# Weighting the experts' hidden layer straight from PSUM on VectorE, output sum on VectorE, third layer four experts behind

## What is computed

```python
x = x + conv(_ln_c(x), w_qkv, w_out, b_out)        # linear attention, 8 heads of 32
t = tokens(x)                                      # [16, 1024, 128]
z = _ln_t(t)
feat = mean(z, axis=0)                             # over the images: [1024, 128]
w = softmax(feat @ Wr + br)                        # [1024, 8]: one weight per pixel and expert
h = relu(bn(z @ W1[e] + b1[e]))                    # for each of 8 experts, hidden 128
h = relu(bn(h @ W2[e] + b2[e]))
y = sum_e w[:, e] * (h @ Wo[e] + bo[e])
x = t + y
```

## Time and profile before

| | |
|---|---|
| device time, median of 3 runs | 882.08 us (880.58 to 882.58) |
| span of the profiled execution | 879.8 us (first to last instruction; the page has no other time of this execution) |
| TensorE busy | 814.8 us, 93% |
| VectorE busy | 738.1 us, 84% |
| ScalarE busy | 575.7 us, 65% |
| GpSimd busy | 340.3 us, 39% |
| mean granted TensorE clock | 0.979 |
| chain of waits: TensorE, VectorE, ScalarE | 52%, 13%, 2% |

### The profile page before, as it was taken

One profiled execution on the slowest core, in us unless ns is written; L12 is line 12 of the kernel. 1 busy time (PEld: TensorE's weight loads), 2 busy tenths in 40 slices (PEclk: granted clock), 3 DMA queues, 4 the chain that ended last, 5 costly groups with the idle time before them and its releaser, 6 DMA issues.

```text
span 879.8 us, 12875 instructions
## 1 busy us (share of the span) xinstructions
PE 814.8 (93%) x4170; PEld 673.9 (77%) x4170; DVE 738.1 (84%) x1165; ACT 575.7 (65%) x650; POOL 340.3 (39%) x377
## 2 busy tenths in 40 slices
PE   5899999999998898899999999999898998999997
PEld 4899999999975677687877878777686776877775
DVE  5678888888866788989898898988989889898887
ACT  2456566666555676767767767676676767767665
POOL 5548787878753221404123041331403214042120
PEclk8999999999999999999999999999999999999999
DMA  7133434343422501201011010110101002010000
GB/s 223 49 121 144 144 137 150 134 152 111 155 96 89 200 24 48 72 1 72 8 63 72 0 72 0 72 58 13 72 0 72 35 37 72 0 72 24 24 25 24
DMA packets 22107, 64.52 MB, mean 73 GB/s; under 512 B 2608, under 2 KB 6840, under 8 KB 22080
## 3 DMA queue, kind: packets, MB, share of 16 engines
q1 hardware_dynamic: 22080, 64.19, 20.4%
HBM read 38.98 MB, written 25.20 MB: 73 GB/s over the span
## 4 chain that ended last, share of the span: by engine, by line
PE 52%; DVE 13%; issue 3%; ACT 2%; POOL 0%; DVEq 0%; ACTq 0%; POOLq 0%
PE psum L515 51%; DVE h_lo L899 9%; DVE w_raw L893 3%; ACT h L691 2%; DVE st L849 0%; PE psum L472 0%; PE psum L566 0%; DVE xn2T L779 0%; POOL ln L989 0%; DVE h_lo L882 0%; POOL xn2T L997 0%; DVE x_res L954 0%; DVE w_raw L933 0%; ACT h_hi L698 0%; PE psum L424 0%
## 5 line engine op out<-in xcount | busy, mean ns | idle before, releaser
L899 DVE TENSOR_TENSOR h_lo<-w_raw,h_hi 128x1024 fp32r<-128x1024 f32 x128 | 219.3, 1714 | 1.1 <-ACT h_hi L698 1.1
L684 ACT ACTIVATE h_hi<-psum 128x1024 fp32r<-128x1024 f32 x128 | 131.5, 1027 | 122.7 <-PE psum L515 122.7
L515 PE MATMUL psum<-h_hi,w_hi 128*128 128x512 f32 x510 | 164.9, 405 | 41.0 <-DVE h_lo L899 41.0
L882 DVE SCALAR_TENSOR_TENSOR h_lo<-psum,h_hi 128x1024 fp32r<-128x1024 f32 x128 | 156.4, 1222 | 42.0 <-ACT h_hi L684 41.7
L1040 POOL TENSOR_TENSOR x_res<-y_out,x_res 128x1024 f32<-128x1024 f32 x15 | 41.1, 2737 | 380.3 <-ACT y_out L734 380.3
L893 DVE TENSOR_TENSOR w_raw<-h,route_all 128x1024 f32<-128x1024 f32 x127 | 160.1, 1261 | 30.5 <-ACT h L691 30.5
L691 ACT ACTIVATE h<-psum,t 128x1024 f32<-128x1024 f32 x128 | 143.1, 1118 | 49.1 <-PE psum L515 49.1
L515 PE MATMUL psum<-h_lo,w_hi 128*128 128x512 f32 x510 | 164.1, 404 | 0.0
L515 PE MATMUL psum<-h_hi,w_lo 128*128 128x512 f32 x510 | 162.9, 401 | 0.0
L515 PEld LDWEIGHTS psum<-h_hi,w_hi 128*128 128x128 f32 x510 | 94.4, 190 | 74.5 <-DVE h_lo L899 51.8
L698 ACT CAST h_hi<-w_raw 128x1024 fp32r<-128x1024 f32 x128 | 132.9, 1039 | 1.6 <-DVE w_raw L933 1.2
(11 more groups left out here) (130 smaller groups left out, 1159.7 us busy)
## 6 DMA issues: line engine op xcount, KB each, us to landing
route_all<-in_x SPq DMA_DIRECT2D x16, 512.0 KB, 4.1
x_res<-in_x SPq DMA_DIRECT2D x16, 512.0 KB, 3.4
x_scratch<-x_res SPq DMA_DIRECT2D x16, 512.0 KB, 2.9
xn_scratch<-xn SPq DMA_DIRECT2D x16, 512.0 KB, 2.6
xs_in<-xn_scratch SPq DMA_DIRECT2D x16, 512.0 KB, 4.5
x_res<-x_scratch SPq DMA_DIRECT2D x16, 512.0 KB, 3.3
out<-x_res SPq DMA_DIRECT2D x15, 512.0 KB, 2.6
route_all<-route_scratch SPq DMA_DIRECT2D x6, 512.0 KB, 6.6
```

What stands on the lines that cost most here:

```text
L515: mm = pe.matmul(dst[:, px], w[:, which, e, :], part[:, px], start=first and w is w_hi and part is hi, stop=last and part is lo, skip_grou ...
L684: nc.scalar.activation(h1_hi[r][:], z1[r], ACT.Relu).then_inc(h1_hi_done, 1)
L882: nc.vector.scalar_tensor_tensor(out=h1_lo[r][:], in0=z1[r], scalar=0.0, in1=h1_hi[r][:].bitcast(F32), op0=ALU.max, op1=ALU.subtract).then ...
L899: nc.vector.tensor_tensor(h2_lo[r][:], h2w[r], h2_hi[r][:].bitcast(F32), ALU.subtract).then_inc(h2_lo_done, 1)
```

## The change

It does this:

- `hidden2` is gone. `weigh` reads z2 in PSUM and makes max(z2, -t2) * route in one scalar_tensor_tensor on VectorE. Since max(z, -t2) = relu(z + t2) - t2, the third layer lacks t2 * route @ Wo; it is put back in the bias: `shifts_through_wo` (8 small matmuls, once) gives t2 @ Wo of each expert, and `bo_full` = bo + that is used in place of bo. Layer2 of a slot now waits for `weigh` of the slot before (h2w_done).
- In the bridge z2 of experts 0 and 1 is copied to SBUF by ScalarE (`z2_out`), since no routing weights exist yet; the product for the bias goes to y's banks and the order is another.
- The output sum is one VectorE tensor_tensor from PSUM at the head of the fifth slot of an image; ScalarE's copy of y and GpSimd's `finish` are gone. Layer3 of the next image waits for it (out_done).
- layer3 runs four slots behind, and h2w, h2_hi and h2_lo are rings of four, which use tiles of the attention stage.
- GpSimd keeps `split_low` and `bias_x1`, now in its own loop over slots; it also makes -t2 and the operand of the 8 small matmuls.

The diff, without the constants and the list of semaphores:

```diff
--- before.py
+++ after.py
...
@@ -72,7 +72,8 @@
     SLOTS = IMAGES * EXPERTS
-    L3_LAG = 3
+    L3_LAG = 4
+    RING = 4
     SPREAD = 2
     BRIDGED = 4
     x1_dram = nc.dram_tensor("x1_scratch", [IMAGES, C, PIXELS], F32, kind="Internal").ap()
@@ -97,7 +98,10 @@
         w_lo = sb("w_lo", [128, 3, EXPERTS, 128], F32R)
         ident = sb("ident", [128, 128])
         t2 = sb("t2", [HIDDEN, EXPERTS])
+        minus_t2 = sb("minus_t2", [HIDDEN, EXPERTS])
+        t2_diag = sb("t2_diag", [HIDDEN, EXPERTS, EXPERTS + 1])
         bo_sb = sb("bo_sb", [EXPERTS, C])
+        bo_full = sb("bo_full", [EXPERTS, C])
         wr_sb = sb("wr_sb", [C, EXPERTS])
         br_sb = sb("br_sb", [128, EXPERTS])
         feat = sb("feat", [128, CHUNKS, C])
@@ -231,13 +235,11 @@
         xs_lo = [sb(f"xs_lo{p}", [C, PIXELS], F32R) for p in range(2)]
         h1_hi = [sb(f"h1_hi{p}", [HIDDEN, PIXELS], F32R) for p in range(2)]
         h1_lo = [sb(f"h1_lo{p}", [HIDDEN, PIXELS], F32R) for p in range(2)]
-        h2 = [sb(f"h2_{p}", [HIDDEN, PIXELS]) for p in range(2)]
-        h2w = [w_raw[:, p].rearrange("p e h -> p (e h)") for p in range(2)]
-        h2_hi = [sb(f"h2_hi{p}", [HIDDEN, PIXELS], F32R) for p in range(2)]
-        h2_lo = [sb(f"h2_lo{p}", [HIDDEN, PIXELS], F32R) for p in range(2)]
-
-        y_out = sb("y_out", [C, PIXELS])
-        feat_most = y_out
+        z2_early = [sb(f"z2_early{p}", [HIDDEN, PIXELS]) for p in range(2)]
+        feat_most = sb("feat_most", [C, PIXELS])
+        h2w = [w_raw[:, p].rearrange("p e h -> p (e h)") for p in range(3)] + [feat_most[:]]
+        h2_hi = [sb(f"h2_hi{p}", [HIDDEN, PIXELS], F32R) for p in range(2)] + xn_hi
+        h2_lo = [sb(f"h2_lo{p}", [HIDDEN, PIXELS], F32R) for p in range(2)] + xn_lo
         z1, z2, y = [banks(4, 2), banks(6, 2)], banks(0, 2), banks(2, 2)
         xs_loaded = [sem(f"xs_loaded{p}") for p in range(2)]
...
@@ -398,6 +401,8 @@
                     mm.then_inc(m_done, 1)
                 if b:
                     turn_e(t, 0, 0)
+                if at(t, 0):
+                    shifts_through_wo()
                 if s:
                     pe.wait_ge(in_loaded[p], 8 * t + (24 if p else 32))
@@ -463,6 +468,14 @@
                                    start=False, stop=True)
                 mm.then_inc(shift_done, 1)
+            def shifts_through_wo():
+
+                pe.wait_ge(t2_ready, 1)
+                for e in range(EXPERTS):
+                    mm = pe.matmul(p_g[0:EXPERTS, 256:384], t2_diag[:].rearrange("p e f -> p (e f)")[:, 8 * e:8 * (e + 1)],
+                                   w_raw[:, 2, e, :], start=e == 0, stop=e == EXPERTS - 1)
+                mm.then_inc(wo_t2_done, 1)
+
             def turn(dst, chunk):
                 return turn_part(dst, 128, chunk)
@@ -500,6 +513,8 @@
             def add_g(t, p, j, h):
                 pe.wait_ge(e_moved, 4 * t + 2 * j + h + 1)
+                if isinstance(t, int) and t == j == h == 0:
+                    pe.wait_ge(bo_full_done, 1)
                 for n in range(4):
                     chunk = 4 * h + n
                     mm = pe.matmul(p_g[:, 128 * j:128 * (j + 1)], xnT[p][:, chunk, :], ekT[j][:, chunk, :],
@@ -525,15 +540,20 @@
             def layer2(s, k):
                 pe.wait_ge(h1_lo_done, s + 1)
-                wait(pe, h2_done, s)
+                if isinstance(s, int) and s <= 2:
+                    wait(pe, z2_moved, s)
+                else:
+                    pe.wait_ge(h2w_done, s)
                 layer(z2, 1, k % EXPERTS, h1_hi[k % 2], h1_lo[k % 2], True, True).then_inc(l2_done, 1)
             def layer3(s, k, image):
-                e, r = (k - L3_LAG) % EXPERTS, (k - L3_LAG) % 2
+                e, r = (k - L3_LAG) % EXPERTS, (k - L3_LAG) % RING
                 pe.wait_ge(h2_lo_done, s - L3_LAG + 1)
-                if e == 0:
-                    wait(pe, y_out_moved, image)
+                if isinstance(s, int) and s == L3_LAG:
+                    pe.wait_ge(bias_moved, 1)
+                elif e == 0:
+                    pe.wait_ge(out_done, image)
                 if isinstance(s, int) and s == SLOTS - 1 + L3_LAG:
                     for n in range(2):
@@ -571,17 +591,13 @@
             turn_part(y, EXPERTS, lambda n: route[:, n, :]).then_inc(routeT_done, 1)
             turn(z1[0], lambda n: route[:, n, 0:1].to_broadcast([128, 128])).then_inc(spread, 1)
+            layer2(2, 2)
             pe.wait_ge(routeT_moved, 1)
             turn(y, lambda n: route[:, n, 1:2].to_broadcast([128, 128])).then_inc(spread, 1)
-
-            pe.wait_ge(h2_done, 2)
+            pe.wait_ge(spread_moved[1], 1)
             for n in range(2):
-                mm = pe.matmul(z2[:, BANK * n:BANK * (n + 1)], bo_sb[:], routeT[:, BANK * n:BANK * (n + 1)], start=True, stop=True)
+                mm = pe.matmul(y[:, BANK * n:BANK * (n + 1)], bo_full[:], routeT[:, BANK * n:BANK * (n + 1)], start=True, stop=True)
             mm.then_inc(bias_done, 1)
-            pe.wait_ge(spread_moved[1], 1)
-            layer3(3, 3, 0)
-            pe.wait_ge(bias_moved, 1)
-            layer2(2, 2)
             pe.wait_ge(spread_moved[0], 1)
             def slot(s, k, image):
@@ -683,18 +699,16 @@
                 wait(act, l2_done, s - 1)
                 nc.scalar.activation(h1_hi[r][:], z1[r], ACT.Relu).then_inc(h1_hi_done, 1)
-            def hidden2(s, k):
-
-                r, e = k % 2, k % EXPERTS
+            def z2_out(s):
+
                 act.wait_ge(l2_done, s + 1)
-                wait(act, h2w_done, s - 1)
-                nc.scalar.activation(h2[r][:], z2, ACT.Relu, bias=t2[:, e:e + 1]).then_inc(h2_done, 1)
+                nc.scalar.copy(z2_early[s][:], z2).then_inc(z2_moved, 1)
             def h2_high(s, k):
-                r = k % 2
+                r = k % RING
                 act.wait_ge(h2w_done, s + 1)
-                wait(act, l3_done, s - 1)
+                wait(act, l3_done, s - RING + 1)
                 nc.scalar.copy(h2_hi[r][:], h2w[r]).then_inc(h2_hi_done, 1)
             rounds(act, step)
@@ -703,39 +717,31 @@
             h1_high(0, 0)
             last_round(step, IMAGES + 1)
             h1_high(1, 1)
-            hidden2(0, 0)
+            z2_out(0)
             act.wait_ge(turned, 1)
             nc.scalar.mul(feat_most[:], p_chan, 1.0 / IMAGES).then_inc(feat_most_moved, 1)
             h1_high(2, 2)
             act.wait_ge(feat_moved, 1)
             last_round(step, IMAGES + 2)
-            hidden2(1, 1)
+            z2_out(1)
             act.wait_ge(step_done, 3)
             nc.scalar.activation(grown[:].rearrange("p n e -> p (n e)"), shifted[:].rearrange("p n e -> p (n e)"), ACT.Exp).then_inc(grown_done, 1)
+            h1_high(3, 3)
             act.wait_ge(routeT_done, 1)
             nc.scalar.copy(routeT[:], y[0:EXPERTS, :]).then_inc(routeT_moved, 1)
-            h2_high(0, 0)
+            act.wait_ge(spread, 1)
+            nc.scalar.copy(route_all[:, 0, :], z1[0]).then_inc(spread_moved[0], 1)
             act.wait_ge(spread, 2)
             nc.scalar.copy(route_all[:, 1, :], y).then_inc(spread_moved[1], 1)
+            h2_high(0, 0)
             act.wait_ge(bias_done, 1)
-            nc.scalar.copy(bias_out, z2).then_inc(bias_moved, 1)
-
-            nc.scalar.copy(route_all[:, 0, :], z1[0]).then_inc(spread_moved[0], 1)
-            h1_high(3, 3)
-            hidden2(2, 2)
+            nc.scalar.copy(bias_out, y).then_inc(bias_moved, 1)
             h2_high(1, 1)
             def slot(s, k, image):
-                if k % EXPERTS == 3 and exists(s - EXPERTS):
-
-                    act.wait_ge(l3_done, s - 3)
-                    wait(act, out_done, image - 1)
-                    nc.scalar.copy(y_out[:], y).then_inc(y_out_moved, 1)
                 if exists(s):
                     h1_high(s, k)
-                if exists(s - 1):
-                    hidden2(s - 1, k - 1)
                 if exists(s - 2):
                     h2_high(s - 2, k - 2)
                 if k % EXPERTS == 4 and exists(s + EXPERTS):
@@ -808,6 +814,9 @@
                     ins.then_inc(y_moved, 1)
                 if b:
                     head_max(t, 1)
+                if at(t, 0):
+                    dve.wait_ge(wo_t2_done, 1)
+                    nc.vector.tensor_tensor(bo_full[:], p_g[0:EXPERTS, 256:384], bo_sb[:], ALU.add).then_inc(bo_full_done, 1)
                 if f and not b:
                     halves(1, x1_tokens(t - 2), t - 2)
                 if c:
@@ -884,19 +893,31 @@
             def weigh(s, k):
-                r, e = k % 2, k % EXPERTS
-                dve.wait_ge(h2_done, s + 1)
+                e = k % EXPERTS
+                z = z2
+                if isinstance(s, int) and s < 2:
+                    dve.wait_ge(z2_moved, s + 1)
+                    z = z2_early[s][:]
+                else:
+                    dve.wait_ge(l2_done, s + 1)
                 if isinstance(s, int) and s < EXPERTS:
```

(55 more changed lines are left out.)

9 lines of the change are left out of this document (5 added, 4 removed).

## The result

The changed kernel takes 839.28 us (median of 4 runs, 838.63 to 840.47) against 882.33 us (880.58 to 883.40) of the kernel before in the same comparison: ratio 0.9524 (0.9500 to 0.9547). The forecast was 845, range 833 to 862. The profiled execution took 840.47 us, of which 838.7 are its span.

What follows compares the result with a forecast made beforehand. TensorE bounds it: 4.20 us slots plus 56.2 us of stalls behind VectorE's line 899. Span 879.8 - 35.7 (stage) - 2.0 (bridge) - 1.1 (end) + 1.5 (beginning) = 842.5, plus 2.3 to the median: 844.8, predicted 845, range 833 to 862.

Steps and rivals of the forecast that it cites:

- The stalls: Expert stage: three short waits an image for layer2's bank or y, 1.34 us instead of 3.57; stage loses 35.7 us.
- The weighing: VectorE's max and product read from PSUM: 1.28 us throughout, not stretched beside GpSimd.
- rival 4: VectorE's weighing sets the slot: beyond 1.75 us each 0.1 costs 12 us; at 2.1, 888 us; chance 0.05.
- The floor: Plain expert slot of 18 matmuls: cannot go below 4.20 us, TensorE's own work, so no gain there.
- The bridge: Between routing and slot 5: 2.0 us gained (0.6 to 3.2), least if the clock falls to half here too.
- The end: Behind the last layer2: last layer3 starts at 873.8, not 874.87, gaining 1.1 us (0 to 1.5).
- the beginning: Before the expert stage: eight more small matmuls and two small GpSimd operations lose 1.5 us (0 to 2.3).
- The worst places for the GpSimd operations (1): Expert stage: GpSimd operations block VectorE at worst times, 2.9 us an image, 867 us, or half, 856; chance 0.13.
- A miss (2): Expert stage: one or both GpSimd operations miss h2_low, 0.49 to 0.9 us an image, 833 to 839 us; chance 0.12.
- The clock (3): TensorE's clock halves behind a stall, 1.7 us each time; once an image gives 870 us; chance 0.06.

Runs made afterwards that it cites:

- The two waits on GpSimd: Changed kernel with a wait ahead of split_low and one ahead of bias_x1, each until an h2_low is done: 824.64 us, ratio 0.9362.
- the earlier output sum: Changed kernel with the output sum behind the weighing of the fourth slot, ahead of h2_low, instead of heading the fifth: 830.93 us, ratio 0.9436.
- the fastest kernel: Changed kernel with both the waits ahead of GpSimd's two operations and the output sum one place earlier: 821.34 us, ratio 0.9313.

## Why the prediction was right, and where it was off

**The stalls: right, in place, releaser and size.** Forecast were h2_low at 2.8 us beside split_low and 2.4 beside bias_x1; it is 2.73 and 2.33. Idle time was to be released by the weighing and by the output sum, not by h2_low: so it is. The forecast had 1.34 us an image; it is 0.30 + 0.24 + 0.19 = 0.73 of shown idle time, and 1.51 with 0.26 more a stall, the 0.16 of a record's length and the 0.10 of the slower start that the forecast reads beside the earlier trace rows. To its own stalls it had added only the 0.10. That makes most of 23.3 against 20.5 us. The two waits on GpSimd, which remove the weighing's two (13.9 us of the stage for 15 images, 0.93 an image where 0.24 + 0.19 + 2 x 0.26 is 0.95), and the earlier output sum (8.0 us, 0.53 an image for 0.56) show both causes, each by itself. A slip of hundredths is in the working: 3.36 + 2.40 is 5.76, not 5.72, and 8.0 + 2.40 is 10.40, not 10.38.

The Trainium skill (SBUF — State Buffer, the section on who interferes with whom) has it that VectorE with two SBUF inputs and GpSimd reading SBUF share a port pair as an exclusive lock, and that what starts second waits until the first is over. The trace agrees: h2_low starts at 400.06 inside split_low, which ends at 401.71, and ends itself at 402.79, 1.08 later, as in the earlier trace rows; a whole one takes 1.22.

**The weighing: right.** The earlier trace rows gave 1.284 us; the view of line 907 has a median of 1.274 for 94 of its operations (1.264 to 1.284), beside GpSimd or not:

```profile
L907 DVE SCALAR_TENSOR_TENSOR w_raw<-psum,minus_t,route_all x94: 1264/1274/1284, 289.0 to 826.8; 128x1024 f32<-128x1024 f32 x94
```

That is far from the 1.75 at which rival 4 begins.

**The floor: wrong.** "A slot cannot go below 4.20, TensorE's own work" failed. It can at the same matmuls, clock and shapes, since the tiles lie elsewhere. This term, put at nothing, is 122 x 0.065 = 7.9 us and the largest error of the sum; shown by the kernel before with unused tiles (6.3 us faster) and by the changed one with 32 bytes more (6.9 slower).

**The bridge: 0.8 instead of 2.0,** inside 0.6 to 3.2, at the end named for a clock that falls here too. It did: granted 0.50 from 288 to 292 us. Layer1(4), whose rows stand below, and layer2(3) behind it run at half pace, pairs 0.85 apart, and the weighing ahead of layer2(3) waits for a routing row as forecast (289.1 reckoned, 288.95 measured), hidden behind the slow layer1. With the two waits on GpSimd, where the clock was 1.00, the same stretch takes 13.0 us, so 3.0 gained for the forecast's 3.2. The timeline of the changed kernel:

```profile
288.58 1.22 PE L530 MATMUL psum<-xs_hi,w_hi 128*128 128x512 f32 x2
289.60 1.05 PE L530 MATMUL psum<-xs_hi,w_lo 128*128 128x512 f32 x2
290.46 1.05 PE L530 MATMUL psum<-xs_lo,w_hi 128*128 128x512 f32 x2
```

**The end: 0.2 instead of 1.1.** The last layer2 has no layer1 ahead of it, so it comes early and meets a weighing that is on time for a full slot, as the timeline shows; the forecast had followed VectorE behind this layer2 and not ahead of it:

```profile
826.80 1.28 DVE L907 SCALAR_TENSOR_TENSOR w_raw<-psum,minus_t,route_all 128x1024 f32<-128x1024 f32 x1
...
828.22 0.71 PE L530 MATMUL psum<-h_hi,w_hi 128*128 128x512 f32 x2 [0.88 <-DVE w_raw L907]
```

**The sum.** The span came out 3.8 us below the forecast: 7.9 by the slot's length less 2.8 by the stalls, 1.2 by the bridge and 0.9 by the end, and 0.7 back at the beginning and behind the last layer3 (each rounded). Another 1.7 lie between span and median: 2.3 was added, and the median is only 0.6 above this profile's span. Errors of both signs, the largest one favourable: a hit within 0.7% that hides a term of 1% of which the forecast knew nothing. The hit does not hang on that term alone: with 32 bytes more, at plain slots of 4.20, the changed kernel takes 846.15 us, 1.2 above the forecast. That the other errors nearly cancel is luck.

**The rivals.** The worst places for the GpSimd operations (1) did not occur here; they did once a third operation was put before them, at 0.8 and 1.2 us a time. A miss (2) did not occur by itself, but could be forced, for 14.6 us. The clock (3) stayed at 1.00 from 300 us on, and no stall grew by it.

**What the forecast did not ask: which part earns the gain.** At like places of the tiles it divides so: unused tiles 6.3 us (881.16 to 874.86), layer3 four behind with its rings another 41.0 (to 833.84), and the weighing from PSUM with the output sum on VectorE minus 5.4 (to 839.28); the runs of the kernel before beside these had medians of 881.16, 881.24 and 882.33, so 1 us of it is loose. At slots of 4.20 the last step is minus 9.1 (837.02 to 846.15). ScalarE's 152.6 us of work had been no burden, since TensorE did not wait for it. Where the 5.4 us lie is less sure. The waits name the weighing and the output sum, which now stand in VectorE's queue and free z2 and y there; but the output sum taken back alone gave 0.7 us and the weighing 2.0, within the intervals, and each time the other's stall grew. In the stage, from one traced execution each, the weighing taken back gives 5.2 us and the output sum 1.0, which points to the weighing. What that pair does give is room. h2_low is VectorE's only operation left with two SBUF inputs, and between two of them lies 4.15 - 1.22 = 2.9 us, in which a GpSimd operation of 2.40 fits. By itself it does not fall there; told to, it does, and with the earlier output sum the whole is then 12.5 us below the rings alone at like places. No run put such waits into the kernel with the rings alone, so that this needs the room is argued from the lengths and not shown.

## To carry to other kernels

Before an operation is taken off an idle engine, ask what it released: a PSUM bank that is then freed behind a busy queue can cost more than the copy that freed it. Where two engines block each other, give the one that is off the critical path a wait for the end of the other's operation and find it a gap that it fits; starting later was worth 14.6 us here. And before a gain of 1% or less is put down to an edit that adds tiles, run the old kernel with the same tiles unused.

## What the runs showed of the hardware that was not expected

- The pace of fp32r matmuls depends on where their moving operand lies in SBUF: 4.08, 4.12 or 4.20 us for the same 18 matmuls (0.227 to 0.233 us each, 512 columns), by a shift of 32 bytes, at a granted clock of 1.00, and 1.37 or 1.40 us for 6 of them inside one execution. It is worth 6 to 11 us of 880. Why bytes 128 and 192 of a block of 256 were fast and 0, 32, 96, 160 and 224 slow, the runs don't tell.
- TensorE's clock in the bridge differs between executions and versions whose work there is the same: 0.67 or 1.00 granted over the same 21 us (the two windows above). The four runs of the fastest kernel, 818.58, 820.06, 822.62 and 823.10 us, have mean granted clocks of 0.996, 0.996, 0.990 and 0.988.
